# Attention denominators: VectorE adds two of three key tiles, TensorE sums one group of four streams, ScalarE widens the inverse

## The reference

```python
# layer 0 (group norm ahead of it)
w_attn = softmax(einsum('ncq,nck->nqk', q, k * scale), axis=2)
a = einsum('nqk,nck->ncq', w_attn, v)
out = einsum('oc,bchw->bohw', proj_w, a) + proj_b + x
# layer 1 (position embeddings added to q and k)
scores = einsum('bhqd,bhkd->bhqk', q, k) * scale
attn = softmax(scores, axis=-1)
o = einsum('bhqk,bhkd->bhqd', attn, v)
out = (o @ Wout + bout) + hidden_states
```

## Time and profile before

| | |
|---|---|
| time before, median of 3 runs | 4526.37 us (4523.8 to 4527.9) |
| profiled execution, time | 4527.92 us |
| profiled execution, span | 4526.1 us |
| granted TensorE clock, mean | 0.991 of full |
| blocks of queries | 48 in each of two attention stages |
| one block in the steady part (353.80 us for ten) | 35.38 us |

### The profile page before, as it was taken

One profiled execution on the slowest core, in us unless ns is written; L12 is line 12 of the kernel. 1 busy time (PEld: TensorE's weight loads), 2 busy tenths in 40 slices (PEclk: granted clock), 3 DMA queues, 4 the chain that ended last, 5 costly groups with the idle time before them and its releaser, 6 DMA issues. The chain is left out here.

```text
span 4526.1 us, 87274 instructions
## 1 busy us (share of the span) xinstructions
PE 4293.3 (95%) x32280; PEld 2523.6 (56%) x32280; DVE 3200.0 (71%) x2892; ACT 2747.3 (61%) x2885; POOL 1455.2 (32%) x584
## 2 busy tenths in 40 slices
PE   7998999999999999998999979999999999999999
PEld 4554555555555555554555545555555555555545
DVE  4223888888888888887433348888888888888862
ACT  1112777777777777776011128777777777777750
POOL 0000444444444444444100004444444444444430
PEclk9999999999999999999999999999999999999999
DMA  5334111211112111120444441211112111111216
GB/s 196 128 128 133 24 53 33 64 33 50 42 44 54 36 47 38 49 50 30 163 149 167 139 115 26 65 33 50 42 44 53 36 47 38 49 42 45 61 32 213
DMA packets 234733, 321.69 MB, mean 71 GB/s; under 512 B 12080, under 2 KB 221104, under 8 KB 233648
## 3 DMA queue, kind: packets, MB, share of 16 engines
q1 hardware_dynamic: 214512, 292.54, 22.3%
q10 hardware_dynamic: 20160, 28.32, 1.7%
HBM read 188.69 MB, written 132.12 MB: 71 GB/s over the span
## 5 line engine op out<-in xcount | busy, mean ns | idle before, releaser
L619 POOL TENSOR_TENSOR prob<-prob,mx 128x1056 f32<-128x1056 f32 x576 | 1434.2, 2490 | 2907.7 <-DVE prob L619 2906.3
L766 ACT ACTIVATE prob<-psum_att 128x1152 f32<-128x1152 f32 x1152 | 1294.1, 1132 | 817.1 <-DVE run L851 635.2
L708 PE MATMUL psum_att<-qst,kst 128*128 128x384 f32 x6912 | 1416.7, 348 | 49.2 <-DMA kst<-qk_scratch 27.6
L779 ACT ACTIVATE prob<-prob 128x1152 f32<-128x1152 f32 x1152 | 1288.1, 1163 | 17.3 <-POOL prob L619 17.3
L708 PEld LDWEIGHTS psum_att<-qst,kst 128*128 128x128 f32 x6912 | 1182.4, 190 | 177.9 <-issue 144.8
L721 PE MATMUL psum_att<-prob,vst 128*32 128x384 f32 x13824 | 1234.2, 490 | 4.7 <-ACT prob L779 2.9
L851 DVE TENSOR_TENSOR run<-psum_att,run 128x1152 f32<-128x1152 f32 x768 | 1013.2, 1349 | 222.3 <-PE psum_att L708 222.1
L619 DVE TENSOR_TENSOR prob<-prob,mx 128x1248 f32<-128x1248 f32 x576 | 996.1, 1730 | 155.8 <-ACT mx L773 155.8
L721 PEld LDWEIGHTS psum_att<-prob,vst 128*32 128x32 f32 x13824 | 391.7, 109 | 593.4 <-issue 593.2
L730 PE MATMUL psum_att<-prob,const_sb 128*32 128x384 f32 x6912 | 663.2, 486 | 0.0
L317 PE MATMUL psum<-xc_l,wq 128*128 128x384 f32 x1536 | 505.1, 490 | 10.4 <-DVE hl_l L422 5.3
(11 more groups left out here) (55 smaller groups left out, 1498.0 us busy)
## 6 DMA issues: line engine op xcount, KB each, us to landing
qk_scratch<-hl_l SPq DMA_DIRECT2D x48, 1536.0 KB, 5.6
qst<-qk_scratch SPq DMA_DIRECT2D x192, 384.0 KB, 5.5
kst<-qk_scratch SPq DMA_DIRECT2D x192, 192.0 KB, 3.3
v_scratch<-vo_l SPq DMA_DIRECT2D x24, 768.0 KB, 3.5
vst<-v_scratch SPq DMA_DIRECT2D x96, 192.0 KB, 2.5
att_scratch<-ob ACTq DMA_DIRECT2D x96, 192.0 KB, 1.9
attc_l<-att_scratch SPq DMA_DIRECT2D x24, 768.0 KB, 5.3
x_sb<-in_x SPq DMA_DIRECT2D x8, 1152.0 KB, 14.2
```

Source lines behind the costliest of these rows:

```text
L619: return engine.tensor_tensor(x, x, m, ALU.subtract)
L708: mm = nc.tensor.matmul(psum[:, 3 * e + k, 0:CH], kst[:, e, (3 * c + k) * P:(3 * c + k + 1) * P], qst[par][:, 2 * w + e, :], start=(w == 0 ...
L766: nc.scalar.activation(chunk_of(par, c, e), s_bank(e), ACT.Copy).then_inc(copied, 1)
L779: nc.scalar.activation(x, x, ACT.Exp, scale=SCALE).then_inc(exp_done, 1)
```

## The change

- The denominators are no longer summed as nine pairs of key tiles. For each group VectorE adds the first two of the three exponentiated tiles into a new buffer `two_tiles` (`pair_tiles`, 128x768 elements, ten groups behind, right after the shift). TensorE's new `add_keys`, eleven groups behind, sums this and the third tile: 4 matmuls a group for all groups.
- The columns of the shift are split at 160 instead of 208, and GpSimd waits for `paired`, so it runs behind VectorE's shift and the addition that stood ahead of it in the count.
- The denominators are copied out of PSUM in slot 5 (`copy_den`), the weighted sums still in slot 4.
- The widening of the inverse moves from VectorE to ScalarE (`widen`), at the end of slot 2.
- Tiles of `prob` come free one group later in odd groups.

```diff
-SHIFT_DVE = 208
-POOL_BEHIND = True
-SHIFT_LAG, EXP_LAG, PV_LAG = 7, 9, 10
+SHIFT_DVE = 160
+SHIFT_LAG, EXP_LAG, PV_LAG, PAIR_LAG, DEN_LAG = 7, 9, 10, 10, 11
-DEN_PAIRS = [[0], [1, 2], [3], [4, 5], [6], [7, 8]]
-FREE_AT = [1, 1, 3, 3, 5, 5]
...
-                for j in DEN_PAIRS[c]:
-                    if j == 0 and not before(t, 1):
-                        pe.wait_ge(den_copied, t)
-                    for e in range(2):
-                        for odd in range(2):
-                            r = 64 * e + 32 * odd
-                            mm = nc.tensor.matmul(psum[r:r + 32, 7, 0:CH], ones[:, :],
-                                                  prob[par][:, e, 2 * j + odd, :], start=(j == 0),
-                                                  stop=(j == KT // 2 - 1), tile_position=(0, r))
-                mm.then_inc(pv_done, 1)
+                return mm
+
+            def add_keys(t, par, c):
+                if c == 0 and not before(t, 1):
+                    pe.wait_ge(den_copied, t)
+                pe.wait_ge(paired, PAIR_LAG - SHIFT_LAG + group(t, c))
+                for e in range(2):
+                    for i, tile in enumerate((two_tiles[c % 2][:, e, :], prob[par][:, e, 3 * c + 2, :])):
+                        r = 64 * e + 32 * i
+                        mm = nc.tensor.matmul(psum[r:r + 32, 7, 0:CH], ones[:, :], tile, start=(c == 0),
+                                              stop=(c == KC - 1), tile_position=(0, r))
+                return mm
...
+                    td, pd, cd = behind(t, par, c, DEN_LAG)
+                    last = None
                     if live(tv):
-                        weigh(tv, pv, cv)
+                        last = weigh(tv, pv, cv)
+                    if live(td):
+                        last = add_keys(td, pd, cd)
+                    if last is not None:
+                        last.then_inc(pv_done, 1)
...
-                    act.wait_ge(pv_done, pv_count(t - 2, FREE_AT[c]))
+                    act.wait_ge(pv_done, pv_count(t - 2, c + 1))
...
+            def copy_den(t):
+                act.wait_ge(pv_done, pv_count(t, KC))
+                if not before(t, 1):
                     act.wait_ge(den_turned, t)
-                nc.scalar.activation(pvr[:, :], pv_bank, ACT.Copy).then_inc(pv_copied, 1)
                 nc.scalar.activation(den[:, :], den_bank, ACT.Copy).then_inc(den_copied, 1)
+
+            def widen(t):
+                act.wait_ge(inverted, t + 1)
+                if not before(t, 1):
+                    act.wait_ge(spread, t)
+                nc.scalar.activation(dwide.rearrange("p r (e i) -> p r e i", e=2),
+                                     dcol[:, :, :].unsqueeze(3).broadcast_to([P, 3, 2, D]), ACT.Copy)\
+                    .then_inc(widened, 1)
...
+                    if c == EVACUATE_AT + 1 and not before(t, 2) and live(t - 2):
+                        copy_den(t - 2)
...
                     if live(te):
                         exponential(te, pe_, ce, 1)
+                    if c == DEN_TURN_AT and not before(t, 3) and live(t - 3):
+                        widen(t - 3)
...
-                        if POOL_BEHIND:
-                            pool.wait_ge(dve_shifted, group(t, c))
+                        pool.wait_ge(paired, group(t, c))
                         shift_part(nc.gpsimd, par, c, SHIFT_DVE, CH).then_inc(pool_shifted, 1)
...
+            dve.sem_inc(paired, PAIR_LAG - SHIFT_LAG)
...
+            def pair_tiles(t, par, c):
+                dve.wait_ge(exp_done, slot(t, c, 1))
+                if c >= 2 or not before(t, 1):
+                    dve.wait_ge(pv_done, pv_count(t, c - 1))
+                nc.vector.tensor_tensor(two_tiles[c % 2][:, :, :], prob[par][:, :, 3 * c, :],
+                                        prob[par][:, :, 3 * c + 1, :], ALU.add).then_inc(paired, 1)
...
-                dve.wait_ge(inverted, t + 1)
-                if not before(t, 1):
-                    dve.wait_ge(spread, t)
-                nc.vector.tensor_copy(dwide.rearrange("p r (e i) -> p r e i", e=2),
-                                      dcol[:, :, :].unsqueeze(3).broadcast_to([P, 3, 2, D])).then_inc(widened, 1)
...
                     if live(ts):
                         shift(ts, ps, cs)
+                    tp, pp, cp = behind(t, par, c, PAIR_LAG)
+                    if live(tp):
+                        pair_tiles(tp, pp, cp)
```

More of the change, by code:

```diff
@@ L546, in attention_stage @@
         den, dsum, dcol, dwide = bufs["den"], bufs["dsum"], bufs["dcol"], bufs["dwide"]
-        pvr, ob = bufs["pvr"], bufs["ob"]
+        pvr, ob, two_tiles = bufs["pvr"], bufs["ob"], bufs["two_tiles"]
         ones, ident = bufs["ones"], bufs["ident"]
@@ L560, in attention_stage @@
         dve_shifted, pool_shifted = sem("dve_shifted"), sem("pool_shifted")
+        paired = sem("paired")
         exp_done = sem("exp_done")
@@ L784, in copy_weighted @@
                     act.wait_ge(normed, t)
+                nc.scalar.activation(pvr[:, :], pv_bank, ACT.Copy).then_inc(pv_copied, 1)
+            def copy_den(t):
+                act.wait_ge(pv_done, pv_count(t, KC))
+                if not before(t, 1):
                     act.wait_ge(den_turned, t)
-                nc.scalar.activation(pvr[:, :], pv_bank, ACT.Copy).then_inc(pv_copied, 1)
                 nc.scalar.activation(den[:, :], den_bank, ACT.Copy).then_inc(den_copied, 1)
+            def widen(t):
[5 more added lines that the diff above has]
+                    .then_inc(widened, 1)
             def store(t, par):
@@ L972, in attention @@
                         "dwide": sb_(c2, nc, f"dwide_{layer}", [P, 3, P]), "pvr": sb_(c2, nc, f"pvr_{layer}", [P, CH]),
-                        "ob": two("ob", [P, CH]), "ones": ones, "ident": ident}
+                        "ob": two("ob", [P, CH]), "two_tiles": two("two_tiles", [P, 2, CH]), "ones": ones, "ident": ident}
                 attention_stage(nc, f"att{layer}", psum, bufs, qk_d, v_d, att_d, next_loads)
```

## The result

The changed kernel takes 4789.7 us against 4526.5, median against median. The ratio is 1.058, with a 95% interval of 1.056 to 1.060. The prediction was 4628, with a range of 4540 to 4730. The direction and the place were right, and the size was not: 263 us were lost and not 101.

A forecast was written before the change was run, and what follows sets the result against it. TensorE's work was taken to bound nearly everywhere, coupled to VectorE at two places. The walk gave a period of 36.52 us against 35.40, 1.12 more in 90 blocks, +101 us: 4628 us, range 4540 to 4730.

The forecast's parts named there:

- T4 = T3 + 5.30: TensorE's start of slot 4 follows its start of slot 3 by 5.30 us, from 5.95 less 0.65.
- The clock is 1.00 in both rows, so it plays no part: Both attention stages before the change: TensorE's granted clock read 1.00, so no clock cost was charged.
- The drain: End of each attention layer, left at zero: few blocks, 0.65 us a slot gained against pair additions.
- slot 5's share: TensorE's denominator matmuls saved in slot 5: not gained, as slot 0's second transpose waits for VectorE's folds, about 0.7 us.
- held shift of slot 0: VectorE's shift in slot 0, held by GpSimd, would take 3.4 us from issue to end.
- The hold: VectorE and GpSimd hold each other; slot 0's held VectorE shift would end at GpSimd's end plus 1.02 us.
- The rule of the lock: Shared VectorE and GpSimd port pair, locked for a whole instruction against VectorE operations with two SBUF inputs.
- rival 1: GpSimd's longer shift part holds nobody: period 35.62 us, +20 us, 4546 us; chance 0.14.
- Rival 2: VectorE's idle time takes up the pair additions: -58 us, 4468 us; chance 0.08.
- Rival 3: VectorE's first fold is held by GpSimd's slot 4 part too: +1.8 us a block more, 4787 us; chance 0.06.
- Rival 4: The widening on ScalarE costs 2.03 us: +1.54 us a block more, 4765 us; chance 0.06.
- The widening's place: ScalarE, behind slot 2's copies and second exponential: slot 3 starts at 24.68 instead of 22.97, TensorE idle 3.8 us.

The follow-up runs named there:

- the filler: Changed kernel with zero-weight matmuls added to the open denominators behind slot 2's streams, in TensorE's wait: 4649.5 us, ratio 1.027.
- The early versions: Changed kernel, and kernel before, each with the widening on ScalarE ahead of slot 2's first copy: 4429.0 us and 4396.9 us.
- the early widening: Widening on ScalarE ahead of slot 2's first copy, not at slot 2's end: changed kernel 4429.0 us, kernel before 4396.9 us.
- the last experiment: Kernel before with the widening on ScalarE ahead of slot 2's first copy, and pair additions for groups 4 and 5 alone: 4365.0 us, ratio 0.964.
- third experiment: Kernel before with only the widening moved to ScalarE, at the end of slot 2, no pair additions: 4702.9 us, ratio 1.039.

## Why the prediction was wrong

The place and the wait were right, and the sum lacked a term: what the wait does to TensorE's clock. The table says where the 264.0 us between the two spans lie. A stage scores from its first to its last score matmul, and its drain lasts from there to the first matmul of the next stage.

| | forecast | after | with the filler |
|---|---|---|---|
| two stages while they score | +101 | +241.4 | +103.5 |
| their two drains | 0 | +23.5 | +19.9 |
| the other three stages | 0 | -0.9 | -1.9 |
| span against before | +101 | +264.0 | +121.5 |

- **The step that failed** is "T4 = T3 + 5.30", together with "The clock is 1.00 in both rows, so it plays no part". The prediction found that TensorE would stand idle 3.8 us (it is 3.62), but charged the idle time alone. Slot 3 takes 6.81 us from T3 to T4 instead of 5.30, since its scores run in part at the lower clock. The filler, which changes nothing but the standstill, brings back 137.9 us in the scoring stretches, 1.53 a period, and 3.6 more in the drains. A clock of 1.00 in the steady part of before says nothing of a kernel whose waits are longer. The trace of before did hold a price, outside the steady part: while the first attention stage fills, TensorE waits 2.52 us for a copy of the scores, and the twelve scores behind it take 4.21 us at a granted clock of 0.50. It is not quite the same case, as TensorE had been busy for only 3.90 of the 6 us from 450 on.

```profile
459.19 4.21 PE L708 MATMUL psum_att<-qst,kst 128*128 128x384 f32 x12 [2.52 <-ACT prob L766]
```

```profile
459.19:463.40 4.21, 4.21 (x12) 3.70 (x12) 2.77 (x3) 4.07 (x4) 2.50 (x2) 0.50 0.00 0
```

- **The drain** was left at zero because its blocks are few and gains stand against pair additions. It costs 11.8 us a stage (10.0 with the filler). The wait of TensorE's streams for the pair addition, put at nothing, is nothing only while a stage scores. All of line 731's 15.2 us of waiting for `two_tiles` on the page lies in the drains. VectorE and GpSimd take turns there and hold each other, here in VectorE's and then in GpSimd's timeline:

```profile
2245.19 1.14 DVE L617 TENSOR_TENSOR prob<-prob,mx 128x960 f32<-128x960 f32 x1
2246.26 3.79 DVE L893 TENSOR_TENSOR two_tiles<-prob 128x768 f32<-128x768 f32 x1
2249.98 1.15 DVE L617 TENSOR_TENSOR prob<-prob,mx 128x960 f32<-128x960 f32 x1
```

```profile
2245.34 3.89 POOL L617 TENSOR_TENSOR prob<-prob,mx 128x1344 f32<-128x1344 f32 x1 [1.96 <-DVE two_tiles L893]
```

An addition of 0.95 us takes 3.79 there, and GpSimd's part 3.89 instead of 3.1. One group takes VectorE 4.79 us there (2245.19 to 2249.98), against 3.03 before (four held shifts from 2117.65 take 12.10). No run changed the drain alone.

- **The denominators' matmuls**: 4608 instead of 6912, as said, and slot 5's share is not gained. The wait for the second fold is 0.55 us (0.7 forecast).
- **The pair addition** takes 0.94 to 0.96 us in a period (0.95 forecast), GpSimd's part 3.05 to 3.10 (3.13), the widening 0.51 (0.49). The held shift of slot 0 takes 3.32 (3.4), that of slot 2 1.39 (1.35). That of slot 4 takes 1.15 and not 1.75: slot 4 comes 1.5 us later than forecast, at 1492.27, and GpSimd's part from 1489.22 is nearly over by then.
- **The hold**: the shift issued at 1465.20 ends at GpSimd's end plus 1.01 (1.02 forecast). The rule of the lock stands; rival 1 falls. The early versions show what additions and holds cost together. Both have a period of 34.0 us (with the kernel before 33.99, from 1405.62 to 1439.61), so in a period they take all of the 1.95 us of matmuls that are saved. The changed kernel with the early widening is 32 us slower than the kernel before with the same, and 18.2 us of that lie in the two drains (115.2 against 97.0).
- **Rival 2**, idle time that takes up the additions, falls for the change as a whole. For the two groups of the last experiment it holds in part: they gain 32 us.
- **Rival 3**, a held fold, gives 4787 and the time is 4790, but it is not what happened. The fold at 1458.16 takes 1.48 us while GpSimd runs from 1456.38 for 3.09. A time that fits is no proof of its mechanism. **Rival 4** falls: 0.51 us.
- **The widening's place** was named as the trouble, and the runs show it to be larger than all the rest: 361 us between two places a few instructions apart. The prediction found T3 to 0.01 us in this period, which is closer than its terms are known (the widening ended 0.15 us ahead of TensorE's start and not 0.05, and the maximum of slot 2 came 0.11 early). It then priced the 1.7 us by which slot 3 starts later, without what the longer standstill does to the scores.

What stays open is what sets how much slower the scores get. They took 3.35 to 4.19 us behind nearly the same waits in the changed kernel, and 8 of 90 periods of the third experiment were spared.

## What to carry to other kernels

When a walk shows that TensorE will stand still longer than it ever did in the trace at hand, price the work behind the standstill at the lower clock as well, as a second end of the range at least. Here waits of about 2 us were followed by it in 82 of 90 periods. Look for such a wait in the trace at hand, also outside the steady part, and if the wait can't be avoided, try filling it with matmuls that change nothing. When a small operation moves to another engine, its place in that engine's order counts for more than its duration: put it where that engine waits anyway. Vector work that relieves TensorE gained here in two slots where VectorE had idle time, and not when it stood in all six; VectorE's share of the whole span did not tell that.

## What the runs showed of the hardware that was not expected

- At the head of slot 3 the score matmuls were slow behind waits of 3.42 to 3.63 us (the change, all 90 periods) and of 1.98 to 2.07 us (third experiment, 82 of 90). They were not slow behind waits of up to 1.61 us (kernel before), 1.48 us (filler) or 0.89 us (early widening). In the middle of the slowed stretch of the period shown the granted clock was 0.50, and the twelve score matmuls took 3.90 us instead of 2.35.
- The hold works in both directions: in the drain GpSimd's own part is stretched too, from 3.1 to 3.89 us, while a VectorE shift runs at its start.
- A reduction and a reciprocal with SBUF operands on VectorE ran beside GpSimd without being held (1.48 and 0.19 us), while an addition, a shift and a copy were held (3.79, 3.32 and 2.99 us).
